# Widening the router gate's matmuls of a gated cross-attention and expert block from 8 to 64 columns

## What is computed

```python
x = x + tanh(g_xattn) * attention(layernorm(x), ctx, ctx)      # per sequence
x = x + tanh(g_ffn) * routed_moe(layernorm(x))

def routed_moe(x):                     # 2048 tokens, 512 features
    logits = x @ gate_w                # (2048, 8): the gate
    top_logits, top_idx = top_k(logits, 2)
    cw = scatter(softmax(top_logits))  # weight of each token for each expert
    return sum(cw[:, e] * ((silu(x @ w0[e]) * (x @ w1[e])) @ wo[e]) for e in range(8))
```

## Time and profile before

| What | Value |
|---|---|
| Median of the runs | 1139.69 us (1136.62 to 1143.68) |
| The profiled execution, its own time | 1138.76 us |
| Its span in the trace | 1136.9 us |
| Mean granted TensorE clock over the span | 0.982 |
| TensorE matmul busy | 1088.6 us, 96% of the span |
| VectorE, ScalarE, GpSimd busy | 804.1, 686.0, 379.3 us |
| Gate matmuls (L307) | 128 records, 15.5 us busy |

### The profile page before, as it was taken

The page is one execution under the profiler, slowest core; times in us unless marked ns, Lnnn a source line. Parts: engine busy times, 40 slices in busy tenths (PEclk is TensorE's granted clock), DMA queues, the critical chain, the costliest instruction groups (busy, mean ns, idle before and its releaser), DMA issues.

```text
span 1136.9 us, 19036 instructions
## 1 busy us (share of the span) xinstructions
PE 1088.6 (96%) x5988; PEld 444.4 (39%) x5988; DVE 804.1 (71%) x1595; ACT 686.0 (60%) x934; POOL 379.3 (33%) x489
## 2 busy tenths in 40 slices
PE   8998999999999999988989999999999999999997
PEld 3322333333333333332344444444444444444443
DVE  7877897888989897889367575657557565764632
ACT  1276777777777777777766474646446464653421
POOL 4572736848384775522220111110111101111001
PEclk9999999999999999999989999999999999999999
DMA  6336535323234323201268685758647586783443
GB/s 200 115 94 185 186 106 189 116 86 107 73 113 134 113 78 104 76 30 61 87 228 274 146 197 107 209 128 218 149 93 204 124 215 147 191 179 56 70 64 47
DMA packets 182671, 150.60 MB, mean 132 GB/s; under 512 B 122672, under 2 KB 144176, under 8 KB 182576
## 3 DMA queue, kind: packets, MB, share of 16 engines
q1 hardware_dynamic: 171680, 128.91, 40.2%
q0 software_dynamic: 7456, 17.57, 7.7%
q10 hardware_dynamic: 3440, 2.94, 1.0%
HBM read 73.80 MB, written 41.23 MB: 101 GB/s over the span
## 4 chain that ended last, share of the span: by engine, by line
PE 78%; DVE 8%; ACT 7%; issue 4%; DMA 2%; SPq 1%; POOL 0%; POOLq 0%; DVEq 0%; ACTq 0%
PE psum L1289 36%; PE psum L1290 10%; PE psum L362 7%; PE psum L349 6%; PE psum L240 5%; ACT W L543 5%; DVE MX L735 3%; PE psum L337 3%; PE psum L289 3%; PE psum L256 2%; PE psum L379 2%; PE psum L307 1%; PE psum L271 1%; ACT W L493 1%; PE psum L277 1%
## 5 line engine op out<-in xcount | busy, mean ns | idle before, releaser
L543 ACT ACTIVATE W<-psum,es 128x512 f32<-128x512 f32 x512 | 321.9, 689 | 72.8 <-PE psum L349 71.3
L735 DVE TENSOR_REDUCE MX<-psum 128x2 f32<-128x1024 f32 x256 | 310.5, 1219 | 52.5 <-PE psum L337 50.1
L1289 PE MATMUL psum<-W,xT 128*128 128x512 f16 x1248 | 273.7, 379 | 0.0
L1289 PEld LDWEIGHTS psum<-W,xT 128*128 128x128 f16 x1248 | 121.5, 98 | 148.5 <-issue 2.9
L349 PE MATMUL psum<-stg 50*128 50x512 f16 x512 | 143.6, 393 | 20.8 <-ACT W L543 16.3
L1562 POOL DMA_INDIRECT out<-yb,target x34 | 53.2, 1563 | 291.4 <-ACT yb L1391 288.9
L1494 DVE TENSOR_TENSOR hh<-sg,psum 128x512 f32<-128x512 f32 x68 | 46.4, 686 | 143.6 <-ACT sg L1378 143.4
L1289 PE MATMUL psum<-W,hT 128*128 128x512 f16 x648 | 144.3, 379 | 0.0
L362 PE MATMUL psum<-W 128*32 128x512 f32 x1024 | 141.5, 625 | 0.0
L1378 ACT ACTIVATE sg<-psum,i 128x512 f32<-128x512 f32 x68 | 46.3, 681 | 143.0 <-PE psum L1289 120.4
L618 DVE SCALAR_TENSOR_TENSOR W<-stg,scw,W 128x1024 f16<-128x1024 f32 x96 | 117.3, 1280 | 12.0 <-ACT W L611 12.0
(11 more groups left out here) (241 smaller groups left out, 1366.5 us busy)
## 6 DMA issues: line engine op xcount, KB each, us to landing
stg<-in_w SPq DMA_DIRECT2D x16, 2048.0 KB, 9.1
stg<-in_wo SPq DMA_DIRECT2D x8, 2048.0 KB, 10.2
stg<-scr SPq DMA_DIRECT2D x183, 64.0 KB, 2.3
Xs<-zero SPq DMA_DIRECT2D x40, 264.0 KB, 3.3
scr<-W SPq DMA_DIRECT2D x32, 256.0 KB, 3.0
W<-W SPq DMA_DIRECT2D x60, 128.0 KB, 2.1
xs<-in_x SPq DMA_DIRECT2D x8, 512.0 KB, 4.1
out<-xs SPq DMA_DIRECT2D x8, 512.0 KB, 3.1
```

The costliest lines, as they stand in the source:

```text
L543: act.activation(m.Pb[:, c % 2, hh, :], m.psT[tile % 2], ACT.Exp, scale=m.es[:, hb // 2:hb // 2 + 1]).then_inc(S["exped"], 1)
L735: dve.tensor_reduce(m.MX[:, hb % 2, c0:c0 + 9:8], m.psS[tile % 2], AX_X, ALU.max, negate=True).then_inc(S["maxed"], 1)
L1289: return pe.matmul(out, rows, m.wh[(e % 2, w)][:, wp, cols], start=start, stop=stop)
```

## The change

Each gate matmul takes the same eight columns of `gw` eight times in a row, through a view with a repeating dimension, and writes 64 columns of PSUM in place of 8. The first group of 128 tokens fills columns 0 to 63 of the bank, the second columns 64 to 127. VectorE reads columns 0 to 7 of each half; the other copies are never read. The number and the order of instructions on every engine, their waits and the data that is loaded stay as they were.

```diff
     def logits(b):
+
         pe.wait_ge(S["router"], 16 * 7)
         for i in range(2):
             evacuated(pe, S, ("f", 2 * b + i))
             for k in range(4):
-                last = pe.matmul(m.psM[:, 8 * i:8 * i + 8], m.xTr[:, i, k * 128:k * 128 + 128], m.gw[:, k, :], start=(k == 0), stop=(k == 3))
+                last = pe.matmul(m.psM[:, 64 * i:64 * i + 64].rearrange("p (r e) -> p r e", r=8), m.xTr[:, i, k * 128:k * 128 + 128],
+                                 m.gw[:, k:k + 1, :].to_broadcast([128, 8, 8]), start=(k == 0), stop=(k == 3))
         last.then_inc(S["logits"], 1)
```

```diff
     def logits(b):
         dve.wait_ge(S["logits"], b + 1)
-        empties(dve.tensor_scalar(m.L[:, :, :], m.psM[:, 0:16].rearrange("p (i e) -> p i e", i=2), 2.0 ** -10, None, ALU.mult), S, ("l", b))
+        empties(dve.tensor_scalar(m.L[:, :, :], m.psM[:, 0:128].rearrange("p (i r) -> p i r", i=2)[:, :, 0:8], 2.0 ** -10, None, ALU.mult), S, ("l", b))
```

## The result

The changed kernel takes 1134.64 us (median of 20 runs, 1131.29 to 1137.7), the kernel before in the same comparison 1138.26 us (20 runs, 1135.53 to 1147.78). The ratio is 0.9961, with a 95% interval of 0.995 to 0.9973: a small gain, 3.6 us by the medians and 4.4 us by the ratio, inside 1%. The forecast was 1135.3 us, 4.4 us under a median of 1139.69 us that rested on three runs.

The account below looks back on a forecast made before the run. TensorE was taken to bound the first stage, slowed by clock falls after gate jobs. Passes 0, read-out 0 and five falls -4.4 us took the 1139.69 us median to 1135.3 us, range 1131 to 1141.

Parts of the forecast that it names:

- What bounds the stage, and where the clock is lost: Attention stage: TensorE, 96% busy, sets the pace; five clock falls to 0.50 for 3.4 us each begin near gate jobs.
- That the gate's near-empty passes bring the falls: Gate jobs: 16 eight-column passes stream too little; with 64 columns all five gate falls go, worth 4.4 us.
- The first rival: Gate slot: something other than the empty passes brings the falls, so they stay; 1139.7 us, chance 0.14.
- The price of a fall, 0.8 to 1.1 us: Gate's first pass to first rank pass, with a fall against without; five falls together 4.4 us.
- Two terms: Gate-to-rank savings forecast for single falls: 0.92 us for the first gate fall, 0.86 for the fourth.
- the one reference of 12.83 us: Gate to rank at 426.31 us, the job without a fall, used as the no-fall time for the others.
- Cost of the wide passes: 0: 128 gate passes: 55 ns of streaming disappear under the 113 ns weight load, so they cost nothing.
- the two-sided argument from the 8- and 256-column passes: Gate and value passes: load and stream run side by side, so a pass takes the longer, not their sum.
- the 0.4 that I had named: End of each gate job: the last pass streams in the open, 48 ns x 8 jobs, 0.4 us at most.
- Falls behind true pauses stay: Falls at 103.4 and 519.8 us, after TensorE was really idle: they stay or move with the phase of things.
- The turn to the experts: 0: Last fall, 10 us long, at the turn: TensorE is not on the chain there, so cost and gain are 0.
- Nothing is given back: Rival at the gate falls: TensorE's gain is whole, 1.7 us each, 8.5 us, 1131.2 us; chance 0.10, shared with more falls saved.

Follow-up runs that it names:

- fillers: Narrow gate on the base, two matmuls of 384 fp16 zero columns ahead of each group's four passes; 1137.58 us, ratio 0.9984 against the kernel before.
- half wide: The change on the base, with the narrow gate matmul kept for odd sequences; 1139.72 us in a single run, then 1137.96 us over ten, ratio 0.9987.
- base: Kernel before, with the experts' loop step numbers checked against their bounds as loaded, gate still narrow; 1140.16 us, ratio 1.0006 against the kernel before.

## Why the prediction was right, point by point

**What bounds the stage, and where the clock is lost.** Right. TensorE's time is what moved: the experts start 5.8 us earlier, the end comes 5.6 us earlier, so from there on only 0.2 us is given back.

**That the gate's near-empty passes bring the falls.** Right, and now shown by dose (16, 32 and 64 columns) and by substitute (fillers); half wide points the same way. The first rival, that the falls stay, is out. What it is in an almost empty pass that lets the clock fall is not shown, only that more streaming, of either kind, makes falls rarer. The Trainium skill's "TensorE: Matmul & The Clock Gate", in its table of why this matters for kernels, is no full account of these falls: there a drop in mid-kernel comes from idle gaps between bursts, while here it comes behind a stretch that is busy throughout by its records. The falls at true pauses agree with it in kind; the longest single pause in the 3.2 us before the fall at 103.4 us is 0.92 us (at 99.83 us), and the kernel after has a pause of 0.82 us at 511.7 us without a fall.

**The price of a fall, 0.8 to 1.1 us.** Right in size on average, for a short fall. The comparison of runs gives it independently, if roughly, since they were not all run side by side: the 20 runs of the changed kernel have a mean clock of 0.9936, the 92 runs of the kernel before beside the experiments 0.9844 at a mean of 1139.5 us, against 1134.7 us. The 0.0092 of the clock between them are 6.1 falls of 3.4 us, and 4.9 us of time: 0.80 us a fall (0.72 by the 4.4 us of the ratio). In the profiled pair the five gate falls gave 3.5 us where I had 4.4. So the forecast of 4.4 us was met in part by luck: a fall is worth less than I said, and over the runs the worth of more than five of them goes. Two terms are short: the first by 0.22 us, and the fourth, 0.22 in place of 0.86. The step that was off is the one reference of 12.83 us for four different phases. Without a fall, and with the narrow gate, the first phase took 13.05 us (base, from 162.44 us) and the fourth 13.48 (half wide, from 360.72 us). In the fourth TensorE waits 1.10 us for `mT` at 362.47 us, where I had expected 0.49. What stands behind this is a hold-up of VectorE. VectorE around the fourth gate in the kernel before, then VectorE and GpSimd in the kernel after:

```profile
361.61 0.62 DVE L742 TENSOR_SCALAR m<-MX 128x16 f16<-128x16 f32 x1
```

```profile
357.88 0.59 DVE L744 TENSOR_SCALAR m<-MX 128x16 f16<-128x16 f32 x1
```

```profile
357.29 1.15 POOL L467 TENSOR_TENSOR W<-W 128x512 f16<-128x512 f32 x1
```

The small instruction at L744 takes 0.18 us in the median; here it ends just as GpSimd's does (358.47 and 358.44 us). In a trace of 64 columns on the base the same line takes 1.21 us beside a GpSimd instruction of 1.26. The Trainium skill, "SBUF — State Buffer", on the two separate sides of the memory, says that VectorE and GpSimd share a pair of ports as an exclusive lock; the rows fit that, but no run here took GpSimd's work away, so the cause of the longer wait is argued and not shown. The same instruction is held up in this phase in the kernel before too (0.62 us at 361.61), where TensorE, at half clock, had nothing to wait for. How long it is held differs from trace to trace: 0.59 to 1.21 us in those read.

**Cost of the wide passes: 0.** Nearly. The passes keep their pace (1.70 us before and 1.72 after for 15 steps), as the two-sided argument from the 8- and 256-column passes said. But the end of a job is in the open: the next group starts 1.93 us after the job's start in place of 1.89, 0.04 us x 8 = 0.3 us, of the 0.4 that I had named and then counted as hidden. 12.87 us from gate to rank, against 12.83 in the one undisturbed phase of before, says the same. The record of a pass grew by 21 ns and not by my 48; the pace did not depend on it. The two paces that my argument leaned on were a little high: from start to start the value passes are 0.216 us apart and the L240 passes 0.429, against my 0.229 and 0.45.

**Falls behind true pauses stay.** Wrong for the profiled execution. Over the traces they come and go: both are there at 102 and 515 us in another trace of the same kernel, neither in the base, whose gate is narrow. So the change is not what removed them. The profiled clock of 0.994 in place of my 0.988 to 0.99 is their absence, and a fall at the turn of 6.8 us in place of 10.2.

**The turn to the experts: 0.** Right: the clock is at 0.50 from 579 us on, and from the last transpose of maxima (L265, at 540.54 us before and 534.56 after) to the experts' first pass (596.44 and 590.61) it is 55.90 us before and 56.05 after.

**Nothing is given back.** Out, by the traces: waits for VectorE take back about half. They appear in the kernel after where the falls had covered them: TensorE's L240 waits 0.67 us for `mT` behind the first gate, where it had waited for nothing at half clock.

## What to carry to other kernels

A tiny matmul under a full-size weight load looks busy in a trace, though little streams in it (by the prediction's estimate 7 of 113 ns here); when several stand in a row, look at the granted clock just behind them. Widening the moving side by a repeating view was free here up to 64 columns and cost 13.8 us at 256: judge it by the pace of the passes. Price a low clock by the same piece of work with and without it, in the same phase, not by half its length, and compare kernels by their mean clock over many runs, since a single trace shows only one draw.

## What the runs showed of the hardware

What I had not expected is that the falls are a matter of chance: the same narrow gate job is followed by one in 12 of 20 cases, and in the kernel before and in the base, whose attention stage is the same, they stand behind another five of seven jobs. Doubling the columns from 8 to 16 changed nothing (0.985, 0.984), doubling again to 32 nearly all (0.992). A fall that began at a gate lasted 10.2 us twice (at 490.3 us in the base, at 489.1 us with 16 columns), with TensorE 9.65 of 10.00 us busy at 1.2 GHz; the one in the base cost 3.9 us, more than three short ones by my price. That length was seen only in the phase in which no query or key projection follows the gate; that this is the reason was not tried. One of 6.8 us stood behind a narrow gate in another phase (from 363.0 us, the single run of half wide) and cost about 2.0 us (15.46 from gate to rank, against 13.48 for a narrow gate without a fall in the same phase).
